# Row blocks of a tile moved into the middle of the next tile's full-array products, and the spent waits taken out

## The reference

```python
Kf = jnp.einsum('bjd,ed->bje', F, K_w)
S = jnp.einsum('bid,bjd->bij', F, Kf)
out = jnp.einsum('bij,ijd->bid', S, W)
out = out + jnp.einsum('bid,ed->bie', F, Q_w)
```

## Time and profile before

| | |
|---|---|
| three runs | median 606.97 us (606.81 to 610.09) |
| the profiled execution | 606.42 us, of which the span from its first to its last instruction is 604.6 us |
| mean granted TensorE clock | 0.998 of 2.4 GHz |
| TensorE busy | 596.4 us (99%) |
| VectorE, ScalarE busy | 399.2 us, 401.5 us (66% each) |
| DMA | 138.12 MB, 228 GB/s over the span |

### The profile page before, as it was taken

How to read it: one execution, slowest core, us unless ns; L and a number is a source line. 1 busy time by engine, 2 the same in 40 slices (tenths; PEclk the granted TensorE clock), 3 DMA queues, 4 the chain that set the end, 5 groups by cost and what they waited for, 6 DMA issues and landing times.

```text
span 604.6 us, 17904 instructions
## 1 busy us (share of the span) xinstructions
PE 596.4 (99%) x7690; PEld 526.3 (87%) x7690; DVE 399.2 (66%) x412; ACT 401.5 (66%) x696; POOL 0.2 (0%) x4
## 2 busy tenths in 40 slices
PE   9999999999999999999999999999999999999995
PEld 7888989889898898988989898898988989889895
DVE  6556768567685675947749475685756768567486
ACT  7888393874938659295692947939387493865920
POOL 0000000000000000000000000000000000000000
PEclk9999999999999999999999999999999999999999
DMA  8644847457575575755657566484754857557177
GB/s 338 262 141 160 330 165 282 183 185 305 191 281 172 210 266 208 279 196 210 242 192 287 203 238 249 143 319 174 277 209 173 318 179 284 173 209 273 70 281 279
DMA packets 29452, 138.12 MB, mean 228 GB/s; under 512 B 3264, under 2 KB 3776, under 8 KB 21312
## 3 DMA queue, kind: packets, MB, share of 16 engines
q1 hardware_dynamic: 20736, 75.83, 31.8%
q10 hardware_dynamic: 8640, 61.15, 28.4%
HBM read 69.86 MB, written 67.11 MB: 227 GB/s over the span
## 4 chain that ended last, share of the span: by engine, by line
PE 98%; DVE 1%; issue 1%; DVEq 0%
PE ps L509 20%; PE ps L447 20%; PE ps L449 19%; PE ps L448 19%; PE ps L541 18%; DVE o_sb L372 1%; PE ps L576 1%; DVEq L49 0%; DVE o_sb L382 0%; PE ps L467 0%; PE ps L465 0%; PE ps L469 0%; DVE f_hi L388 0%; DVEq L115 0%
## 5 line engine op out<-in xcount | busy, mean ns | idle before, releaser
L337 DVE TENSOR_TENSOR f_lo<-f_ring,f_hi 128x1024 fp32r<-128x1024 f32 x124 | 151.8, 1224 | 168.2 <-ACT f_hi L217 166.6
L231 ACT ACTIVATE q_out<-ps 128x512 f32<-128x512 f32 x256 | 156.9, 613 | 6.6 <-PE ps L449 0.2
L222 ACT ACTIVATE kf<-ps 128x512 f32<-128x512 f32 x256 | 155.8, 609 | 3.5
L372 DVE TENSOR_TENSOR o_sb<-ps,q_out 128x1024 f32<-128x1024 f32 x127 | 145.1, 1215 | 19.4 <-PE ps L541 19.3
L240 ACT ACTIVATE s_t<-ps 128x512 f32<-128x512 f32 x32 | 19.1, 598 | 175.8 <-PE ps L509 175.8
L509 PE MATMUL ps<-f_ring,kf 128*64 128x64 f32 x4096 | 123.5, 222 | 0.3 <-issue 0.3
L509 PEld LDWEIGHTS ps<-f_ring,kf 128*64 128x64 f32 x4096 | 121.1, 138 | 2.6 <-issue 0.8
L541 PEld LDWEIGHTS ps<-s_t,w_sb 64*128 64x128 f32 x2048 | 115.6, 188 | 5.6 <-issue 5.6
L541 PE MATMUL ps<-s_t,w_sb 64*128 64x128 f32 x2048 | 118.6, 274 | 0.0
L447 PE MATMUL ps<-f_hi,k_hi 128*128 128x512 f32 x255 | 101.0, 396 | 0.0
L447 PE MATMUL ps<-f_hi,q_hi 128*128 128x512 f32 x256 | 100.0, 391 | 0.0
(11 more groups left out here) (39 smaller groups left out, 160.3 us busy)
## 6 DMA issues: line engine op xcount, KB each, us to landing
out<-o_sb SPq DMA_DIRECT2D x127, 512.0 KB, 3.5
f_ring<-f_t ACTq DMA_DIRECT2D x58, 1024.0 KB, 4.8
f_ring<-f_t SPq DMA_DIRECT2D x4, 1024.0 KB, 10.6
f_ring<-f SPq DMA_DIRECT2D x8, 256.0 KB, 5.3
w_sb<-w SPq DMA_DIRECT2D x1, 2048.0 KB, 17.8
out<-o_sb SPq DMA_DIRECT2D x2, 256.0 KB, 2.6
o_sb<-first SPq DMA_DIRECT2D x1, 192.0 KB, 2.9
o_sb<-first ACTq DMA_DIRECT2D x1, 192.0 KB, 3.4
```

Of the source, the lines that this page charges most:

```text
L222: nc.scalar.activation(kf[:, c // 2, c % 2 * CK:(c % 2 + 1) * CK, :, :].rearrange("d k h i -> d (k h i)"), ps[:, 2 * c % 8, :], COPY).then ...
L231: nc.scalar.activation(q_out[:, t % 2, :, :].rearrange("d i (h b) -> d i h b", h=2)[:, :, :, at:at + CK], q_bank(t * CHUNKS + c).rearrange ...
L337: nc.vector.tensor_tensor(f_lo[:, v % SPLIT, :], f_unit(v), f_hi[:, v % SPLIT, :].bitcast(F32), ALU.subtract).then_inc(flo_done, 1)
L372: nc.vector.tensor_tensor(o_sb[:, n % OBUF, :, :, :].rearrange("d x s b -> d s x b"), ps[:, bank:bank + 2, :].rearrange("d s (x b) -> d s ...
```

## The change

1. The row blocks of tile t stand no longer behind the 16 chunks of tile t+1 but behind its chunk 7 (`MID = 8`). The order on TensorE is then: scores of t, chunks 0 to 7 of t+1, the eight row blocks of t, chunks 8 to 15 of t+1, scores of t+1. The row blocks of tile 15 stay at the end.
2. The waits follow: row blocks 0 to 3 wait for the copies of chunks 4 to 7, chunks 8 to 11 for the sums of row blocks 4 to 7 (`out_done`), and the scores of every tile for the copies of chunks 12 to 15.
3. DVE's eight `sum_out` of tile t stand behind `both_f(v + 6)` and ahead of `low_f(v + 7)`, `both_f(v + 8)` and `low_f(v + 9)`.
4. The spent waits are gone.

```diff
-FILL = {1: 0, 2: 56}
-FILL.update((t, 108) for t in range(3, TILES - 1))
-FILL[TILES - 1] = 132
+MID = 8
...
                 both_f(v + 6)
+                for k in range(UNITS):
+                    sum_out(t, k)
                 low_f(v + 7)
                 both_f(v + 8)
                 low_f(v + 9)
-                for k in range(UNITS):
-                    sum_out(t, k)
...
             def scores_tile(t):
                 for e in range(UNITS):
-                    if t == 0:
-                        pe.wait_ge(kf_copied, max(2 * e + 2, 13 + e // 2))
-                        if e % 2:
-                            pe.wait_ge(q_copied, 13 + e // 2)
...
-                    elif e % 2 == 0:
-                        pe.wait_ge(out_done, (t - 1) * UNITS + 5 + e // 2)
+                    pe.wait_ge(kf_copied, t * CHUNKS + max(2 * e + 2, 13 + e // 2))
+                    if e % 2:
+                        pe.wait_ge(q_copied, min(t * CHUNKS + 13 + e // 2, TILES * CHUNKS - LATE))
...
                     elif t < TILES - 1:
-                        pe.wait_ge(kf_copied, (t + 1) * CHUNKS + 13 + k)
-                        pe.wait_ge(q_copied, min((t + 1) * CHUNKS + 13 + k, TILES * CHUNKS - LATE))
+                        pe.wait_ge(kf_copied, (t + 1) * CHUNKS + MID - 3 + k)
+                        pe.wait_ge(q_copied, (t + 1) * CHUNKS + MID - 3 + k)
...
-                    if c >= 4:
+                    if t >= 1 and MID <= c < MID + 4:
+                        pe.wait_ge(out_done, (t - 1) * UNITS + 5 + c - MID)
+                    elif c >= 4:
                         pe.wait_ge(kf_copied, n - 3)
...
-                    if c >= 4:
+                    if 4 <= c < MID or c >= MID + 4 or c >= 4 and t == 0:
                         pe.wait_ge(q_copied, n - 3)
                     if t < TILES - 1 or c < CHUNKS - LATE:
                         q_product(n)
-                    if t >= 1:
-                        for x in range(FILL[t] * c // CHUNKS, FILL[t] * (c + 1) // CHUNKS):
-                            pe.wait_ge(zeros_done, 1)
+                    if t >= 1 and c == MID - 1:
+                        rows_tile(t - 1)
...
             for t in range(TILES):
                 scores_tile(t)
                 if t < TILES - 1:
                     project(t + 1)
-                rows_tile(t)
+            rows_tile(TILES - 1)
```

More of the change, by code:

```diff
@@ L470, in k_halves @@
                 ins.then_inc(k_done, 1)
[L472 to L484, removed]
-                    if c >= 4:
[L487 to L491, removed]
-                    if c >= 4:
-                        pe.wait_ge(q_copied, n - 3)
-                    if t < TILES - 1 or c < CHUNKS - LATE:
-                        q_product(n)
-                    if t >= 1:
-                        for x in range(FILL[t] * c // CHUNKS, FILL[t] * (c + 1) // CHUNKS):
-                            pe.wait_ge(zeros_done, 1)
             def scores(t, e):
@@ L514, in scores_tile @@
                 for e in range(UNITS):
-                    if t == 0:
-                        pe.wait_ge(kf_copied, max(2 * e + 2, 13 + e // 2))
-                        if e % 2:
-                            pe.wait_ge(q_copied, 13 + e // 2)
-                        if e == 0:
-                            for c in range(2):
-                                pe.wait_ge(f_first[c], 16)
-                    elif e % 2 == 0:
-                        pe.wait_ge(out_done, (t - 1) * UNITS + 5 + e // 2)
+                    pe.wait_ge(kf_copied, t * CHUNKS + max(2 * e + 2, 13 + e // 2))
+                    if e % 2:
+                        pe.wait_ge(q_copied, min(t * CHUNKS + 13 + e // 2, TILES * CHUNKS - LATE))
+                    if t == 0 and e == 0:
+                        for c in range(2):
+                            pe.wait_ge(f_first[c], 16)
                     scores(t, e)
@@ L571, in rows_tile, with project @@
                     row_block(t, k)
+            def project(t):
+                for c in range(CHUNKS):
+                    n = t * CHUNKS + c
+                    if n == 0:
+                        k_halves()
+                        pe.wait_ge(qlo_done, 1)
+                        q_product(n)
+                        continue
+                    if n < PIECES:
+                        pe.wait_ge(flo_first, n + 2)
+                    elif n % 2 == 0:
+                        pe.wait_ge(flo_done, n // 2 - FIRST + 1)
+                    if t >= 1 and MID <= c < MID + 4:
+                        pe.wait_ge(out_done, (t - 1) * UNITS + 5 + c - MID)
+                    elif c >= 4:
+                        pe.wait_ge(kf_copied, n - 3)
+                    elif t >= 1:
+                        pe.wait_ge(s_copied_act if c % 2 else s_copied, (t - 1) * 2 + c // 2 + 1)
+                    k_product(n)
+                    if 4 <= c < MID or c >= MID + 4 or c >= 4 and t == 0:
+                        pe.wait_ge(q_copied, n - 3)
+                    if t < TILES - 1 or c < CHUNKS - LATE:
+                        q_product(n)
+                    if t >= 1 and c == MID - 1:
+                        rows_tile(t - 1)
             pe.wait_ge(zeros_done, 1)
```

## The result

The changed kernel takes 621.14 us in the median (621.03 to 621.60, 4 runs), the one before 607.29 beside it (4 runs): a ratio of 1.0219, 95% interval 1.0189 to 1.0249. It is 13.9 us slower. The forecast was 617.5, slower, with a range of 608.5 to 623.

What follows compares the result with a forecast made beforehand. TensorE was taken to bound the kernel, busy 596.4 of 604.6 us. A tile grows 0.75 us, fifteen times +11.3, less 0.7 won back in the scores: +10.6, so 617.5 us, range 608.5 to 623.

Steps and rivals of the forecast that it cites:

- The mechanism: VectorE's first sum stands behind `both_f(v+6)`, begins 0.84 us late, and TensorE's chunk 8 waits 0.55 us for sum 4.
- The wait in the row blocks: Row blocks to chunk 8 take 7.90 us instead of 7.35, with the first sum 2.05 us behind the first row matmul.
- The changes of kind: Switches on TensorE between scores, products and row blocks: four a tile instead of three, net +0.20 us for 15 tiles.
- The stalls won back: Scores of tiles 2 and 3, 0.54 and 0.17 us longer than later ones, return to 7.61: 0.7 us gained.
- Stores beside the load: Load behind chunk 7 overlaps the first stores for 1.6 us; room of about 0.9 us should take it, priced at nothing.
- a sign of being wrong: Listed for the profile after: TensorE not waiting in the row blocks, scores longer than 7.7 us, or sums waiting for stores.
- Rival 2: Load delays stores by more than 0.9 us, sums 5 to 7 and chunks 9 to 11 wait: 632; chance 0.05.
- The spent waits: TensorE's extra waits cost 0.03 us a tile at most; removing them is worth nothing.
- Rival 3: Instructions come late: each scores stage loses 0.54 us as the stages' places in the instruction stream move: 626; chance 0.12.
- The sum: A tile takes 37.72 us against 36.97, +0.75; fifteen times +11.3, less 0.7 for scores: +10.6 us.
- the forecast's own range: 612 to 621 us: from +0.5 us a tile, half the wait hidden, to +1.0, weight loads exposed; chance 0.68.
- the wider one: 608.5 to 623 us, the range widened to hold 8 in 10.

Runs made afterwards that it cites:

- the same program: Changed kernel with VectorE's eight sums ahead of `both_f(v + 6)` and the loads behind chunks 2, 13 and 15 in place of 3, 7 and 11: 633.26 us.
- the shifted one: Kernel before, with 108 spent waits in tile 1 too, so later stages begin 53 instructions further into a block of 256: 624.49 us, ratio 1.0284.
- The best of the new order: Changed kernel with the sums ahead of `both_f(v + 6)` and the loads behind chunks 2, 5 and 11 in place of 3, 7 and 11: 610.21 us.
- the first run here: Changed kernel with one thing moved: VectorE's eight sums ahead of the cast and subtraction of unit v+6: 618.33 us, ratio 1.0188.

## Why the prediction was right, and where its terms were off

- **The mechanism.** Predicted: TensorE waits in the row blocks since VectorE's first sum stands behind `both_f(v+6)`. Shown: take that away and the row blocks are 7.35 us, add 1.26 us to it and they are 9.31.
- **The wait in the row blocks.** Predicted 7.90 us for the stage, measured 8.06. The first sum was put at 2.05 us and came at 2.16, as the first sum does not overlap the subtraction ahead of it (198.12 + 1.23 = 199.35, start 199.38); the 0.09 of overlap was that of the sums among themselves. The rest is the time from sum to product: chunk 8 started 0.16 us after sum 4's end (199.38 + 4 x 1.13 + 1.22 = 205.12), not 0.11. The stage is 0.16 us longer than predicted, 15 x 0.16 = 2.4 us, the term that was most off.
- **The changes of kind.** The unknown, rows to products, was bounded by scores to products, 0.20, and is 0.20 (0.09 + 0.11) where nothing waits. In the changed kernel itself, behind the wait, the first product holds TensorE for 0.30 us (205.28 to 205.58), not for the 0.34 foreseen. The second half of the products was put at 11.08, measured 11.09.
- **The stalls won back.** 0.7 us predicted, 0.8 measured, as tile 6 of before had 7.75 us too. Scores are 7.61 or 7.62 in all tiles but the last, which has 7.72 in both kernels: right.
- **Stores beside the load.** Priced at nothing, with about 0.9 us of room: 0.2 us in each of two tiles. The sums did wait for stores, six times, which the prediction had named as a sign of being wrong; it hardly mattered. That it hardly mattered was luck: the very lateness that costs 0.7 us a tile gives the stores their room, which the text did not see. Rival 2 was priced as if it stood alone; it is worth 8.1 us when the sums are on time.
- **The spent waits.** "Their removal is worth nothing" is right for this change (621.67 with them) and would have been wrong by 8.6 us for the order before. Rows of tile 1 and of a later tile show that they take no time, which is not what they are worth. Rival 3 named the mechanism, and what it put against itself, that the stores are gone from beside the scores, is what kept it away: with loads in their place the same program stalls.
- **What was not seen.** From the last tile's row blocks to the end are 14.3 us before (590.30 to 604.6) and 16.1 after (603.24 to 619.3): 1.7 us that the sum did not speak of. The stores of that stretch land 4.7 to 5.2 us after issue, and 2.7 to 3.7 before:

```profile
DMA to landing us min/median/max: 2.7/3.2/3.7
```

```profile
DMA to landing us min/median/max: 4.7/4.9/5.2
```

(the first of before, the second of after). The run without spent waits, whose order is that of before, has 2.9/5.1/5.4 and the shifted one 2.8/4.9/5.2, so it does not come from the move. This stretch takes 15.6 to 16.3 us in the profiles of all ten experiments, and 14.3 in that of before alone. Why stays open.

The sum: 10.6 predicted, plus 2.4, plus 0.4 and 1.7 makes 15.1. Small terms the other way (chunks 0 to 7 at 11.11 us for 11.13, 15 times, and 0.1 more won back in the scores) bring it to the 14.7 by which the profiled executions differ (621.17 less 606.42 is 14.75). The medians differ by 13.9, and 621.14 lies just above 612 to 621, the forecast's own range, and inside the wider one.

No version tried beats the kernel before. The best of the new order is 610.2 us, and the 0.21 us a tile that it keeps is the added change of kind, which belongs to the order.

## What to carry to other kernels

When work moves into the middle of something, ask what the engine that drains it is doing at that moment: here a margin of 0.40 us in one place of VectorE's program decided 11 us, with VectorE 65% busy. After taking a wait away, look for the one that it covered, before reading the total as a verdict; the first run here would have spoken against a theory that was right. And padding in an instruction stream has to be judged with the dense stage and the traffic beside it: it was worth 7.5 us in the scores of one order and nothing in the other.

## What the runs showed of the hardware

- Once in every 256 instructions TensorE can stall for want of instructions, in a stage in which it takes an instruction every 15 ns (7.46 us for 512): by 0.3 to 1.2 us in 13 tiles of the kernel without spent waits, with 311 GB/s of DMA traffic beside it where it was read (tile 2). With 2 to 7 GB/s beside it the scores of the changed kernel have no stall at any of 16 places, and the same program with 181 GB/s beside tile 5 has 1.4 us.
- Where the scores stall depends on the place to within a matmul, and in steady tiles it is the same each time: 1.28 us (8.90 less 7.62) behind matmul 248 in most tiles of the shifted kernel. With 221 GB/s beside it a tile at another place has none.
- Half-array work to full-array products costs 0.20 us (0.09 ahead of the first product, 0.11 in it), the other way 0.09 and, into row blocks, 0.10 more for the first pair.
- A wait of TensorE costs more than its length: of 0.71 us lost in the row blocks of a tile the view of waits has 0.3. Behind each pause of 0.24 us the next one is 0.21, where 0.105 is usual.
